# Attention in blocks of eight score units before the weighted sums of two groups, text units ahead of them inside the block, and a ring of 18 exps

## What is computed

```python
h = tokens(x, W)                       # (8, 1024, 64)
h = concat([h, txt], axis=1)           # 8 batches, 1024 + 32 = 1056 tokens, 64 features
q, k, v = split(layernorm(h) @ w_qkv + b_qkv)      # 8 heads of 8 features
dots = einsum('bhid,bhjd->bhij', q, k) * 64 ** -0.5
attn = softmax(dots, axis=-1)          # over the 1056 keys
h = h + einsum('bhij,bhjd->bhid', attn, v) @ w_out + b_out
```

## Time and profile before

| what | value |
|---|---|
| time, median of 3 runs | 2459.3 us (2456.57 to 2460.78) |
| the profiled execution | 2457.84 us, span 2456.1 us |
| mean granted clock of TensorE, share of full | 0.873 |
| first score unit to last copy of sums | 216.8 to 1046.5 us |
| exps, row maxima in that stage | 1104, 512 |
| busy in the whole span: PE, DVE, ACT | 2022.6, 1307.7, 1126.0 us |

### The profile page before, as it was taken

One profiled execution on the slowest core, in us unless ns is written; L12 is line 12 of the kernel. 1 busy time (PEld: TensorE's weight loads), 2 busy tenths in 40 slices (PEclk: granted clock), 3 DMA queues, 4 the chain that ended last, 5 costly groups with the idle time before them and its releaser, 6 DMA issues. The chain is left out here.

```text
span 2456.1 us, 43798 instructions
## 1 busy us (share of the span) xinstructions
PE 2022.6 (82%) x16356; PEld 921.0 (37%) x16356; DVE 1307.7 (53%) x3427; ACT 1126.0 (46%) x2103; POOL 215.6 (9%) x243
## 2 busy tenths in 40 slices
PE   6848999999999998947599999707649995899998
PEld 2311222222222222246344444303219983454444
DVE  2458877788878886001344444377783442333231
ACT  1313777677776776600245444304313320445544
POOL 1110000000000000000000000033100233000000
PEclk9956999999999998665699999958859995899999
DMA  5440111111111100021100000000000000000000
GB/s 217 140 88 2 29 25 39 28 25 29 25 37 29 25 15 12 10 76 70 27 1 1 1 1 1 2 1 1 1 3 2 2 1 23 1 5 10 5 10 10
DMA packets 43166, 63.15 MB, mean 26 GB/s; under 512 B 25580, under 2 KB 28230, under 8 KB 39902
## 3 DMA queue, kind: packets, MB, share of 16 engines
q1 hardware_dynamic: 38378, 51.35, 8.1%
q0 software_dynamic: 3104, 8.72, 0.9%
q10 hardware_dynamic: 1492, 0.46, 0.1%
HBM read 42.80 MB, written 17.71 MB: 25 GB/s over the span
## 5 line engine op out<-in xcount | busy, mean ns | idle before, releaser
L724 ACT ACTIVATE b_prob<-b_p_s 128x512 f32<-128x512 f32 x1104 | 572.6, 597 | 307.5 <-PE b_p_s L839 259.3
L744 DVE TENSOR_REDUCE b_m<-b_p_m 128x1 f32<-128x1024 f32 x512 | 601.2, 1219 | 140.3 <-PE b_p_s L839 121.3
L807 PE MATMUL b_p_m<-b_k,b_q 48*64 48x512 bf16 x2048 | 379.4, 423 | 89.0 <-DMA b_k<-qk_scr 22.4
L839 PE MATMUL b_p_s<-b_q,b_k 51*64 51x512 bf16 x2048 | 368.8, 413 | 2.5 <-ACT b_prob L724 2.5
L867 PE MATMUL b_p_o<-b_prob,v_all 128*9 128x512 f32 x2304 | 325.9, 640 | 0.0
L807 PEld LDWEIGHTS b_p_m<-b_k,b_q 48*64 48x64 bf16 x2048 | 97.9, 109 | 449.8 <-DVE b_m L744 260.3
L1300 ACT ACTIVATE d_hidden<-d_p_z 128x704 f32<-128x704 f32 x192 | 135.5, 754 | 145.0 <-PE d_p_z L1204 144.7
L1300 ACT ACTIVATE n_hidden<-n_p_z 128x704 f32<-128x704 f32 x192 | 135.1, 754 | 126.5 <-PE n_p_z L1204 126.5
L1418 DVE TENSOR_TENSOR d_xg<-d_xd,d_p_c 128x352 f32<-128x352 f32 x192 | 91.4, 517 | 181.1 <-PE d_p_c L1193 181.1
L1418 DVE TENSOR_TENSOR n_xg<-n_xd,n_p_c 128x352 f32<-128x352 f32 x96 | 50.0, 521 | 203.4 <-PE n_p_c L1193 203.4
L1204 PE MATMUL d_p_z<-d_xg,d_w 64*128 64x352 f32 x768 | 144.0, 495 | 0.0
(11 more groups left out here) (342 smaller groups left out, 2495.0 us busy)
## 6 DMA issues: line engine op xcount, KB each, us to landing
xt<-in_x SPq DMA_DIRECT2D x16, 1024.0 KB, 8.7
c_sums<-sum_scr SPq DMA_DIRECT2D x8, 1056.0 KB, 5.8
sum_scr<-b_sums POOLq DMA_DIRECT2D x32, 256.0 KB, 2.3
b_q<-qk_scr SPq DMA_DIRECT2D x96, 66.0 KB
qk_scr<-a_qk_part SPq DMA_DIRECT2D x24, 256.0 KB, 2.8
b_k<-qk_scr SPq DMA_DIRECT2D x16, 198.0 KB
b_k<-qk_scr SPq DMA_DIRECT2D x16, 132.0 KB
out<-hid SPq DMA_DIRECT2D x8, 256.0 KB, 2.6
```

The lines of the kernel that those rows point to most:

```text
L724: nc.scalar.activation(prob[:, U % PR_RING, 0:w], p_s[:, U % S_RING, 0:w], ACT.Exp, scale=float(D) ** -0.5).then_inc(exp_done, 1)
L744: nc.vector.tensor_reduce(m3[:, x, 0:1], p_m[:, s, :, :].rearrange("p k n -> p (k n)"), axis=AX.X, op=ALU.max).then_inc(rows_free, 1)
L807: last = nc.tensor.matmul(out[e:e + 64, k, :], q_st[s][r, i, t * P + e:t * P + e + 64], k_st[s][r, i, k * WIDE:k * WIDE + WIDE], start=Tru ...
L839: last = nc.tensor.matmul(out[e:e + 64, :], k_st[s][r, q, jt * P + e:jt * P + e + 64], q_st[s][r, q, a * WIDE:a * WIDE + WIDE], start=True ...
```

## The change

The two orders are computed in another way. Scores of eight units (two groups) now form a block; a text unit stands in the block ahead of the sums. After a block's scores come the weighted sums of all groups of the block before. The ring of exps grows from 12 to 18 slots, `S_RING` stays at 3 and `p_m` at two. The row stream is 7 rows ahead instead of 8; groups 12 and 14 have one row instead of two, and two rows stand by themselves ahead of the last two units. Text keys come ahead of the first half's text unit, text rows at the ninth group, TURN at the 15th. ACT copies the sums after units 0, 8 and 41 instead of 3, 36 and 66.

```diff
-    PR_RING, S_RING = 12, 3
+    PR_RING, S_RING = 18, 3
...
-        AHEAD = 8
-        ORDER = list(range(FULL_ROWS))
-        ORDER[24:24] = [FULL_ROWS]
-        ORDER[16:16] = [FULL_ROWS + 1, FULL_ROWS + 2]
-        STEPS = []
-        for j in range(NQ):
-            for x in ORDER:
-                if x == TURN_AFTER and j >= 1:
-                    STEPS.append((j - 1, TURN, 0, 1))
-                parts = 2 if x < FULL_ROWS else 1
-                STEPS += [(j, x, k, parts) for k in range(parts)]
-        STEPS.append((NQ - 1, TURN, 0, 1))
-        slot_of = {step[:2]: X for X, step in enumerate(step for step in STEPS if step[2] == 0)}
-        plain = lambda n: STEPS[n][1] < FULL_ROWS
-        FIRST = STEPS.index((1, AHEAD, 0, 2))
-        alone, paired = {}, {}
-        n = FIRST
+        TEXT_KEYS, TEXT_ROWS, TEXT_END = FULL_ROWS, FULL_ROWS + 1, FULL_ROWS + 2
+        HEAD = 7
+        GROUPS = [u for u in range(US) if UNITS[u][0] < 2 and UNITS[u][1] < FULL and UNITS[u][2] == 0]
+        TEXT = [u for u in range(US) if UNITS[u][0] < 2 and UNITS[u][1] == FULL]
+        TAIL = [u for u in range(US) if UNITS[u][0] == 2]
+        BLOCK_END = [u + 3 for u in GROUPS[1::2] if u + 4 not in TEXT] + TEXT + TAIL[-1:]
+        SLOTS, alone, paired = [], {}, {}
+
+        def slot(j, x):
+            if j < NQ:
+                SLOTS.append((j, x))
+            return j < NQ
+
+        def by_itself_at(U, j, x):
+            if slot(j, x):
+                alone[U].append((j, x))
+
+        def paired_at(U, j, x):
+            if slot(j, x):
+                paired[U].append((j, x, 0))
+                paired[U + 1].append((j, x, 1))
+
+        alone[-1] = []
+        for x in range(FULL_ROWS + 3):
+            by_itself_at(-1, 0, x)
+        for x in range(HEAD):
+            if x == 1:
+                by_itself_at(-1, 0, TURN)
+            by_itself_at(-1, 1, x)
         for j in range(NQ):
             for u in range(US):
+                alone[US * j + u], paired[US * j + u] = [], []
+            y = HEAD
+            for n, u in enumerate(GROUPS):
                 U = US * j + u
-                alone[U], paired[U] = [], []
-                regular = UNITS[u][0] < 2 and UNITS[u][1] < FULL
-                while n < len(STEPS) and not plain(n) and regular:
-                    alone[U].append(n)
-                    n += 1
-                if n < len(STEPS) and plain(n) == regular:
-                    paired[U].append(n)
-                    n += 1
-        left = range(n, len(STEPS))
-        pair_of = {slot_of[STEPS[n][:2]]: U for U in paired for n in paired[U] if STEPS[n][2] + 1 == STEPS[n][3]}
+                if n == 8:
+                    by_itself_at(US * j + TEXT[0], j + 1, TEXT_KEYS)
+                    by_itself_at(U, j + 1, TEXT_ROWS)
+                    by_itself_at(U, j + 1, TEXT_END)
+                if n == 14:
+                    by_itself_at(U, j + 1, TURN)
+                for at in range(0, 2 if n in (12, 14) else 4, 2):
+                    paired_at(U + at, j + 1 + y // FULL_ROWS, y % FULL_ROWS)
+                    y += 1
+            for u in TAIL[1:]:
+                by_itself_at(US * j + u, j + 1 + y // FULL_ROWS, y % FULL_ROWS)
+                y += 1
+        slot_of = {step: X for X, step in enumerate(SLOTS)}
+        pair_of = {slot_of[j, x]: U for U in paired for j, x, k in paired[U] if k == 1}
         by_itself = sorted(set(slot_of.values()) - set(pair_of))
...
                     nc.scalar.activation(prob[:, U % PR_RING, 0:w], p_s[:, U % S_RING, 0:w], ACT.Exp, scale=float(D) ** -0.5).then_inc(exp_done, 1)
-                    if u in (END[0] + 3, END[1]):
-                        copy_sums(SUMS * j + (0 if u < END[1] else 1))
-                    if u == 3 and j:
-                        copy_sums(SUMS * j - 1)
+                    if u in (0, 8) and j:
+                        copy_sums(SUMS * j - (2 if u == 0 else 1))
+                    if u == END[0] + 8:
+                        copy_sums(SUMS * j)
+            copy_sums(SUMS * NQ - 2)
             copy_sums(SUMS * NQ - 1)
...
-            for n in range(FIRST):
-                rows_ready(n)
-                rows(n)
+            for j, x in alone[-1]:
+                rows(j, x)
             pe.wait_ge(sums_clear, 1)
-            pending = None
+            pending, block = [], []
             for j in range(NQ):
                 b, p = divmod(j, HG)
                 pe.wait_ge(max_in[p], MAX_IN * (b + 1))
                 lo = 0
                 for u in range(US):
                     U = US * j + u
-                    for n in alone[U]:
-                        rows_ready(n)
-                        rows(n)
-                    for n in paired[U]:
-                        rows_ready(n)
+                    for step in alone[U]:
+                        rows(*step)
+                    for h, x, k in paired[U]:
+                        if k == 0:
+                            rows_ready(h, x)
                     score_ready(U)
-                    for n in paired[U]:
-                        rows(n)
+                    for step in paired[U]:
+                        piece(*step)
                     score(j, u)
                     if u in LAST:
-                        if pending is not None:
-                            weigh(*pending)
-                        pending = (j, lo, u + 1)
+                        block.append((j, lo, u + 1))
                         lo = u + 1
-            for n in left:
-                rows_ready(n)
-                rows(n)
-            weigh(*pending)
+                    if u in BLOCK_END:
+                        for group in pending:
+                            weigh(*group)
+                        pending, block = block, []
+            for group in pending:
+                weigh(*group)
```

More of the change, by code:

```diff
@@ L589, in attend_stage @@
     MS = FULL_ROWS + 3
-    TURN_AFTER = 4
     half_in = [[g.sem(f"b_half_in{s}{q}") for q in range(HG)] for s in range(2)]
@@ L753, in max_parts @@
             def max_parts(j):
-                dve.wait_ge(rows_free, slot_of[j, ORDER[-1]] + 1)
+                dve.wait_ge(rows_free, max(slot_of[j, x] for x in range(MS)) + 1)
                 nc.vector.tensor_reduce(neg_max[:, :], m3[:, :, :], axis=AX.X, op=ALU.max, negate=True).then_inc(max_step, 1)
@@ L776, in _, with rows_ready @@
             nc.vector.memset(p_o[:, :], 0.0).then_inc(sums_clear, 1)
[L777 to L780, removed]
+            left = [MS] * NQ
+            for j, x in SLOTS:
+                if x == TURN:
+                    turned(j)
+                else:
                     row_max(j, x)
-                max_parts(j)
-            turned(NQ - 1)
+                    left[j] -= 1
+                    if left[j] == 0:
+                        max_parts(j)
         @block.tensor
         def _(pe):
-            def rows_ready(n):
-                j, x, k, parts = STEPS[n]
+            def rows_ready(j, x):
                 X = slot_of[j, x]
-                if x == ORDER[0] and k == 0:
+                if x == 0:
                     pe.wait_ge(half_in[j // HG % 2][j % HG], HALF_IN * (j // HG // 2 + 1))
@@ L793, in rows_ready, with piece @@
                     pe.wait_ge(max_step, 6 * j + 6)
-                if k == 0 and X >= 2:
+                if X >= 2:
                     pe.wait_ge(rows_free, X - 1)
-            def rows(n):
-                j, x, k, parts = STEPS[n]
+            def piece(j, x, k):
                 b, p = divmod(j, HG)
@@ L803, in rows @@
                 out = p_m[:, slot_of[j, x] % 2, :, :]
-                if x < FULL_ROWS:
[L805 to L809, removed]
+                i, t = divmod(x, FULL)
+                for e in range(0, P, 64):
+                    last = nc.tensor.matmul(out[e:e + 64, k, :], q_st[s][r, i, t * P + e:t * P + e + 64], k_st[s][r, i, k * WIDE:k * WIDE + WIDE],
+                                            start=True, stop=True)
+                return last
+            def rows(j, x):
+                b, p = divmod(j, HG)
+                s = b % 2
+                r = slice(64 * p, 64 * p + KS)
+                out = p_m[:, slot_of[j, x] % 2, :, :]
+                rows_ready(j, x)
+                if x < FULL_ROWS:
+                    for k in range(2):
+                        last = piece(j, x, k)
+                elif x == TEXT_KEYS:
                     for y in range(FULL_ROWS):
@@ L815, in rows @@
                 elif x < TURN:
-                    for bank, lo, w in [(0, 0, WIDE), (1, WIDE, WIDE)] if x == FULL_ROWS + 1 else [(0, TOK, QN)]:
+                    for bank, lo, w in [(0, 0, WIDE), (1, WIDE, WIDE)] if x == TEXT_ROWS else [(0, TOK, QN)]:
                         for i in range(QUAD):
@@ L822, in rows @@
                         last = nc.tensor.transpose(out[0:ROWS, 0, :].bitcast(BF16)[:, a * P:a * P + P], max_part[:, a, :], g.eye_bf[:])
-                if slot_of[j, x] not in pair_of and k + 1 == parts:
```

(2 more changed lines are left out.)

## The result

| | before | after |
|---|---|---|
| median | 2460.04 us (4 runs, 2456.57 to 2470.73) | 2660.03 us (4 runs, 2633.89 to 2671.76) |
| ratio | 1 | 1.0796, 95% interval 1.0735 to 1.0858 |
| span of the profiled execution | 2456.1 | 2664.5 |
| mean granted clock | 0.873 | 0.816 |
| first score unit to last copy of sums | 216.8 to 1046.5 | 213.9 to 1253.6 |

The change makes the kernel 200 us, 8%, slower; the forecast was 2615, with a range of 2500 to 2690. In the profiled executions all of it lies in the attention stage: it lasts 1039.7 instead of 829.7 us, and what stands behind it takes 1410.9 against 1409.6.

A forecast was written before the change was run, and what follows sets the result against it. No engine was full; the handover between PE, ACT and DVE bounds the attention stage. A quad of 54.4 + 5 x 1.4 = 61.4 us against 51.24, +10.2, x15 = +153, then +4 - 1.2, gave 2615 us, range 2500 to 2690.

The forecast's parts named there:

- The plain block: Eight units and two groups of sums at full clock: 5.54 us, 0.68 longer than two cycles of today, 4.86.
- The quad at full clock: A head quad summed block by block at equal clock: 54.4 us against 49.9 today, +4.5 a quad.
- The ring at nothing: Exps' ring of 18 slots holds a block's exps and those of the block before; costed at nothing.
- The clock: Longer stretches without 512-wide sums make the granted clock fall to 1.2 GHz four to six times a quad, against one.
- five falls of 1.4 a quad: Clock term of the forecast: 5 x 1.4 us added to a quad's 54.4, giving 61.4.
- the bound of 1.8: Upper bound in us on what one fall of the clock costs; 1.4 was taken, lower bound 0.5.
- The ends: Stage's start and last quads: +10.2 for a quad with row work, +4 for the last, -1.2 once before the scores.
- The faster one: Rival: PE's own work is the bound, so fewer entries and exits save 3.1 us a quad: 2409; chance 0.10.
- Full clock (2510): Rival: the clock falls as today or not at all; 2510 us without a fall; chance 0.24, from 2500 to 2562.
- mostly half clock (2720): Rival: falls hold through the next stretch, ten a quad, 68.4 us a quad, +258: 2720; chance 0.10.

The follow-up runs named there:

- e3_again: Changed kernel with matmuls repeated where PE waits (pairs 4 to 6, last pair before text keys, scores after text rows); 2574.89 us, ratio 1.0486.
- e7_half_sums: Changed kernel with the second group's weighted sums of each batch cut from 512 to 32 queries, so sums are incomplete; 2572.91 us.
- e8_half_max: On e3_again, a full row's maximum taken over its first 512 keys instead of 1024, so maxima are partial; 2511.15 us.
- e2_one_group: Changed kernel with one group a block instead of two and ACT's copies of the sums in their old places; 2447.92 us, ratio 0.9947.
- e11_again_end_first: On e3_again, the two text-row steps exchanged, the short one first; 2534.27 us, ratio 1.0310.
- e5_end_first: On e2_one_group, the 32-wide text-row step put ahead of the 1024-wide one; 2432.37 us, ratio 0.9873.
- e1_ring: Kernel before the change with a ring of 18 exps instead of 12, nothing else; 2465.46 us, ratio 1.0010.
- e6_after_end_first: Changed kernel with only the two text-row steps exchanged, the short one first; 2603.25 us, ratio 1.0577.
- e9_last_pairs: On e5_end_first, the last quad's regular score units get row pieces written to a bank nobody reads; 2414.13 us, ratio to before 0.9817.
- e4_before_again: Kernel before the change with pairs of units 2, 3, 5 and 7 repeated and four more scores after the text rows; 2453.12 us, ratio 0.9964.
- e10_before_end_first: Kernel before the change with only the two text-row steps exchanged; 2457.21 us, ratio 0.9984.

## Why the prediction was right, and where it was off
- **The plain block.** 5.54 forecast, 5.48 measured at full clock (e3_again), released as written: pair 4 by ACT, 5 and 7 by DVE. e7_half_sums shows the cause (the pause of PE: 4.68 with a short one), e8_half_max the part of DVE.
- **The quad at full clock.** 54.4 forecast, 54.24 measured with repeated pairs in it and a clock of 0.99; one-group quads 49.9 worked out, 49.88 measured (e2_one_group). +4.5 a quad became +4.3 (e11_again_end_first against e5_end_first). Over 15 quads that is 65 of the 200 us.
- **The ring at nothing**: right (e1_ring).
- **The clock.** The mechanism was right, and the term was too small. The sum took five falls of 1.4 a quad, 7.0; the mean quad lost 65.6 - 54.4 = 11.2, and its clock was 0.78 where about 0.85 was forecast. The number of falls was about right, 5.4 a quad. What I had wrong is how long one holds: I priced each as the 3.4 us of the earlier trace rows, and they held 5.4 us on average and up to 13.7, so that the mean quad has 28.9 us at half clock, and a fall cost 2.1 instead of 1.4, above the bound of 1.8. Per us of half clock the price stayed nearly the same: 11.2 / 28.9 is 0.39, against 1.2 / 3.4, 0.35, in e2_one_group. That a fall makes the next batch long, and the scores behind it lie alone again and hold the clock down, is my reading and not shown; e6_after_end_first, where one place was changed and 9.2 us of half clock a quad went, speaks for it. So 61.4 a quad was 4.2 too low.
- **The ends.** From first pair to first pair, the last two quads take 60.0 each against 58.1 and 54.8 before, in the profiled executions: 7.1 more, where the sum had 10.2 and 4. Both were already long before the change by half clock, which the sum left out; that this took back 7 us of the 14 x 4.2 missing is luck. The first score is 2.9 earlier instead of 1.2. So 2615 was 45 us below the median.
- **The rivals.** The faster one would have needed pair 8 before 2.68: it starts at 3.33. Full clock (2510) is not what happens even when PE is given more work (2534 and 2575), and mostly half clock (2720) is partly what happened: falls did hold through the next stretch, as that rival had it, but only in one quad in three is the clock at half for most of the time (0.69 over 70.6 us).

Why the clock falls is shown only as far as this: more matmuls in its waits made the half clock less in e3_again and e9_last_pairs, but not in e4_before_again, and fewer made it more in e7_half_sums. The longest falls stand at the stage's end, where scores have no piece beside them: 51.2 us before, 58.0 in e4_before_again, e5_end_first and e10_before_end_first. With pieces there (e9_last_pairs) the last quad had none. Whether the pieces keep a fall from beginning or from holding these runs don't tell.

## What to carry to other kernels
Before work is put in longer batches to save switches, compare the length of the batch with what the buffers in front of the other engines hold: here 1.96 us of pause stood against two row banks and three score banks, and saving 12 switches of 0.25 us a quad cost 4.3. A cost of the granted clock must be counted beside the waits; if work is taken off TensorE, part of the gain may be lost again to the clock, and harmless work in its waits can save time, as the last quad shows; it need not, as e4_before_again shows. And look at the last round of a loop: where one of two streams has run dry, it may run at half clock.

## What the runs showed of the hardware
- The granted clock fell again and again (70 times in 13 quads) although PE's longest idle time in the changed kernel's quads is 1.32 us (at the text rows); in e7_half_sums it was at half for 57% of a quad.
- Adding matmuls whose result nobody reads took a stretch of 64.14 us to 44.32 at the same ACT work (36.7 and 36.6 us), while the clock went from 0.56 to 1.00.
- The Trainium skill's page TensorE: Matmul & The Clock Gate, section "Why this matters for your kernels", asks for no long pauses between bursts. The trace doesn't agree that this is enough: the changed kernel has no such pause and runs its quads at 0.69 to 0.86.
- Entering or leaving a batch with another tiling costs about 0.1 us each way, at 9-wide columns against 64-wide: last pair to sums takes 0.31 to 0.34, pair to pair 0.215; a batch of one group lasts 0.98 until the next pair and one of two 1.84, so 0.12 are beyond the 0.86 of a group.
